# Ten row slots and a step-by-step order in a gather-and-scatter graph network kernel

## The reference

```
h = relu(layernorm(x))
# layer 1, twice (relu between, log_softmax behind): norm holds edge weight and degrees
out = segment_sum((h @ W)[src] * norm[:, None], dst) + b
x = x + log_softmax(out)
# layer 2
h = relu(layernorm(x))
msg = relu(h[src] + edge_attr @ We + be)
h = h + segment_sum(msg, dst)
x = x + relu(batchnorm(relu(h @ W1 + b1) @ W2 + b2))
```

## Time and profile before

| what | value |
|---|---|
| time, median of 3 executions | 6395.15 us (6393.17 to 6398.4) |
| span of the profiled execution | 7443.2 us |
| GpSimd (POOL) busy | 4606.9 us, 62% |
| TensorE (PE) busy | 3143.2 us, 42% |
| VectorE (DVE) busy | 1940.5 us, 26% |
| ScalarE (ACT) busy | 882.4 us, 12% |
| mean granted TensorE clock | 0.553 of full |
| DMA | 293.10 MB, 39 GB/s |

### The profile page before, as it was taken

The page is one execution under the profiler, slowest core; times in us unless marked ns, Lnnn a source line. Parts: engine busy times, 40 slices in busy tenths (PEclk is TensorE's granted clock), DMA queues, the critical chain, the costliest instruction groups (busy, mean ns, idle before and its releaser), DMA issues.

```text
span 7443.2 us, 65119 instructions
## 1 busy us (share of the span) xinstructions
PE 3143.2 (42%) x13129; PEld 2504.6 (34%) x13130; DVE 1940.5 (26%) x6985; ACT 882.4 (12%) x3744; POOL 4606.9 (62%) x4769
## 2 busy tenths in 40 slices
PE   5333333333333533333333333355555555555556
PEld 5322222222222522222222222243333334333334
DVE  3222222222222322222222222252222222222223
ACT  3100000000000200000000000031111111111113
POOL 3566666666666366666666666656666666666665
PEclk5555555555555555555555555556666555656656
DMA  1111111111111211111111111122222222221111
GB/s 41 50 34 33 34 34 33 34 34 33 34 34 33 55 34 34 33 34 34 33 34 34 34 33 34 34 62 45 47 46 46 45 46 46 46 45 44 44 44 48
DMA packets 227042, 293.10 MB, mean 39 GB/s; under 512 B 97266, under 2 KB 147464, under 8 KB 226889
## 3 DMA queue, kind: packets, MB, share of 16 engines
q0 software_dynamic: 150144, 230.70, 14.8%
q1 hardware_dynamic: 76870, 62.08, 2.9%
HBM read 273.19 MB, written 19.25 MB: 39 GB/s over the span
## 4 chain that ended last, share of the span: by engine, by line
POOL 32%; issue 28%; another core or an unknown queue 14%; PE 11%; DVE 6%; DMA 4%; ACT 3%; DVEq 2%; POOLq 0%; ACTq 0%; SPq 0%
POOL rows_g L404 32%; PE psum L747 8%; DMA rows_g<-table,idx 4%; DVE hot L1044 3%; PE psum L694 1%; ACT rows_g L542 1%; DVEq L261 1%; PE psum L781 1%; ACT idx L523 1%; DVE rows_g L1061 1%; DVE acc L1052 1%; ACT attr L522 0%; PE psum L725 0%; PE psum L864 0%
## 5 line engine op out<-in xcount | busy, mean ns | idle before, releaser
L404 POOL DMA_INDIRECT rows_g<-table,idx x4692 | 4444.1, 947 | 2603.7 <-issue 1331.2
L747 PE MATMUL psum<-hot,rows_g 128*96 128x128 f32 x9384 | 2208.9, 415 | 3997.2 <-DMA rows_g<-table,idx 2231.7
L747 PEld LDWEIGHTS psum<-hot,rows_g 128*96 128x96 f32 x9384 | 1895.5, 266 | 4376.5 <-issue 3038.6
L1052 DVE TENSOR_TENSOR acc<-acc,psum 96x128 f32 x1173 | 332.2, 283 | 4591.9 <-PE psum L747 2411.2
L522 ACT ACTIVATE attr<-edge 128x12 f32 (+1 forms) x1173 | 248.8, 212 | 5844.4 <-PE psum L747 3503.9
L1041 DVE TENSOR_SCALAR hot<-iota,attr 128x128 f32<-128x128 f32 x3128 | 828.6, 355 | 277.5 <-issue 247.5
L736 PE MATMUL psum<-we_blk,eaT 128*128 128x384 f32 (+1 forms) x782 | 533.9, 854 | 140.7 <-ACT eaT L538 95.2
L736 PEld LDWEIGHTS psum<-we_blk,eaT 128*128 128x128 f32 (+1 forms) x782 | 241.1, 329 | 349.7 <-issue 349.7
L1044 DVE TENSOR_SCALAR hot<-iota,attr 128x128 f32<-128x128 f32 x1564 | 324.4, 302 | 103.1 <-issue 103.1
L1061 DVE TENSOR_TENSOR rows_g<-rows_g,psum 128x384 f32<-128x384 f32 x391 | 213.8, 547 | 277.0 <-DMA rows_g<-table,idx 233.6
L542 ACT ACTIVATE rows_g<-rows_g 128x384 f32<-128x384 f32 x391 | 200.6, 513 | 391.4 <-DVE rows_g L1061 317.7
(11 more groups left out here) (136 smaller groups left out, 840.2 us busy)
## 6 DMA issues: line engine op xcount, KB each, us to landing
rows_g<-table,idx POOLq DMA_INDIRECT x4692
ea<-in_edge_attr_dram SPq DMA_DIRECT2D x390, 64.0 KB
table<-tab SPq DMA_DIRECT2D x13, 840.0 KB
tab<-in_x_dram SPq DMA_DIRECT2D x100, 46.9 KB
x_sb<-in_x_dram SPq DMA_DIRECT2D x1, 4200.0 KB
out_dram<-x_sb SPq DMA_DIRECT2D x5, 840.0 KB
x_more<-in_x_dram SPq DMA_DIRECT2D x3, 840.0 KB
table<-tab SPq DMA_DIRECT2D x13, 97.5 KB
```

Source lines behind the costliest of these rows:

```text
L404: pool.indirect_dma_start(out=rows_g[u][0:np_, g * F:(g + 1) * F], out_offset=None, in_=table[p], in_offset=bass.IndirectOffsetOnAxis(ap=i ...
L747: last = pe.matmul(ps_agg[u], rows_g[u][0:np_, g * F:(g + 1) * F], hot[u][0:np_, g, :], start=g == 0, stop=g == G - 1)
L1052: dve.tensor_tensor(a, a, ps_agg[u], ALU.add).then_inc(fast.added, 1)
```

## The change

The slots become `U = 10` for `rows_g`, `attr` and `idx`, and `H = 5` for `hot` and `ea`; `eaT`, its PSUM tile, the products' and the aggregates' banks become two each. To make room, `ea`, `eaT` and one `hot` lie in `x_more_t`, and `far` and `stat` lie in the space of `rows_g`. A class `Step` names the slot, the bank and the count of a step. Loops run over ten steps in place of three, and within them the order goes step by step:

- VectorE: one-hots of step s+3, then (pass 2) the edge term of s, then a window (of s; in pass 2 of s-1). The one-hots of the first three steps come before the loop. `build_hot` has a new wait, for the aggregate of the step five before.
- TensorE, pass 2: transpose of s+3, product of s+2, aggregate of s.
- ScalarE, pass 2: copy of s+2, relu of s, stage of s+9; in all passes the first ten steps are staged ahead of the loop.
- GpSimd and SyncE: loops of ten steps; x is loaded again by 25 DMAs of four columns in place of 100 of one, and the log-softmax columns go four at a time in the first 25 loops.

```diff
-    U = 3
+    U = 10
+    H = 5
+    LA = 3
+    LT, LL = 3, 2
@@
-        ps_agg = [bank[u][0:F, 0:W] for u in range(U)]
-        ps_e = [bank[3 + u][:, 0:G * F] for u in range(U)]
+        ps_agg = [bank[k][0:F, 0:W] for k in range(2)]
+        ps_e = [bank[3 + k][:, 0:G * F] for k in range(2)]
@@
+        class Step:
+            def __init__(self, it, k):
+                self.it, self.u = it + k // U, k % U
+                self.s = it * U + k
+                self.h, self.b = k % H, k % 2
+                self.ith = it * (U // H) + k // H
@@ scalar
+            def stage_first(p):
+                act.wait_ge(fast.agg, U + p * NS)
+                for k in range(U):
+                    stage_fast(p, Step(0, k))
...
+            def gin_iter(it):
+                for k in range(U):
+                    t = Step(it, k)
+                    gin_copy(Step(it, k + LL))
+                    relu_msg(fast, t.s, t.u, EP)
+                    if k >= 1:
+                        stage_fast(2, Step(it, k - 1 + U))
+                stage_fast(2, Step(it, 2 * U - 1))
@@ tensor
+            with pe.Fori(0, ITERS - 1) as it:
+                for k in range(U):
+                    gin_transpose(Step(it, k + LT))
+                    gin_linear(Step(it, k + LL))
+                    aggregate(2, Step(it, k))
@@ vector
-            def build_hot(p, s, u, np_):
-                dve.wait_ge(fast.staged, p * NS + s + 1)
+            def build_hot(p, t):
+                n = p * NS + t.s
+                dve.wait_ge(fast.staged, n + 1)
+                dve.wait_ge(fast.agg, n + 1 + U - H)
@@
-                    for u in range(us):
-                        build_hot(p, s0 + u, u, np_)
-                    for u in range(us):
+                for k in range(LA):
+                    build_hot(p, Step(0, k))
+                def full(it):
+                    w = windows(dve, mybir.EngineType.DVE, it * U, U, win_row)
+                    for k in range(U):
+                        t = Step(it, k)
+                        build_hot(p, Step(it, k + LA))
                         if p == 2:
-                            add_edge_term(fast, s0 + u, it, u, np_)
-                            if u >= 1:
-                                add_window(p, s0 + u - 1, u - 1, w[u - 1])
+                            add_edge_term(fast, t.s, t.it, t.u, t.b, EP)
+                            if k >= 1:
+                                add_window(p, Step(it, k - 1), w[k - 1])
```

More of the change, by code:

```diff
@@ L238, in build_gnn, with last_steps @@
         far_dsum = sem("far_deg_used")
[L239 to L246, removed]
+        USES = [ITERS + (TP > 0)] + [ITERS] * (U - 1)
+        class Step:
[4 more added lines that the diff above has]
+                self.ith = it * (U // H) + k // H
+                self.np_ = TP if isinstance(it, int) and it * U + k == FULL else EP
+        REST = NS - (ITERS - 1) * U
+        def last_steps(ahead=0):
+            return [Step(ITERS - 1, k) for k in range(ahead, REST)]
         def if_far(eng, sweep):
@@ L645, in _ @@
         def _(pe):
-            for r, n in ((fast, U), (slow, 1)):
-                pe.sem_inc(r.agg, n)
-                pe.sem_inc(r.tr, n)
-                pe.sem_inc(r.lin, n)
+            for r in (fast, slow):
+                pe.sem_inc(r.agg, r.rows)
+                pe.sem_inc(r.tr, r.eas)
+                pe.sem_inc(r.lin, r.banks)
             pe.sem_inc(far_used, 1)
@@ L742, in aggregate, with aggregate_pass @@
                 if p < 2:
[L743 removed]
+                    pe.wait_ge(fast_got[t.u], 16 * G * (p * USES[t.u] + t.it + 1))
                 else:
[L745 removed]
+                    pe.wait_ge(fast.relu, t.s + 1)
                 for g in range(G):
[L747 removed]
+                    last = pe.matmul(ps_agg[t.b], rows_g[t.u][0:t.np_, g * F:(g + 1) * F], hot[t.h][0:t.np_, g, :],
                                      start=g == 0, stop=g == G - 1)
                 last.then_inc(fast.agg, 1)
+            def aggregate_pass(p):
+                with pe.Fori(0, ITERS - 1) as it:
+                    for k in range(U):
+                        aggregate(p, Step(it, k))
+                for t in last_steps():
+                    if t.s == NS - 1:
+                        warm(WARM)
+                    aggregate(p, t)
+                pe.wait_ge(fast.added, fast.banks + (p + 1) * NS)
             def sweep(p):
@@ L788, in _ @@
                     transpose_nodes(0, q)
-            with pe.Fori(0, ITERS) as it:
-                for u in range(U):
-                    aggregate(0, it * U + u, it, u, P)
-            warm(WARM)
-            aggregate(0, FULL, ITERS, 0, TP)
-            pe.wait_ge(fast.added, U + NS)
+            aggregate_pass(0)
             if_far(pe, lambda: sweep(0))
@@ L807, in _ @@
                     transpose_nodes(1, q - LAG)
-            with pe.Fori(0, ITERS) as it:
-                for u in range(U):
-                    aggregate(1, it * U + u, it, u, P)
-            warm(WARM)
-            aggregate(1, FULL, ITERS, 0, TP)
-            pe.wait_ge(fast.added, U + 2 * NS)
+            aggregate_pass(1)
             if_far(pe, lambda: sweep(1))
@@ L869, in _ @@
         def _(dve):
-            for r, n in ((fast, U), (slow, 1)):
-                dve.sem_inc(r.added, n)
-                dve.sem_inc(r.msg, n)
+            for r in (fast, slow):
+                dve.sem_inc(r.added, r.banks)
+                dve.sem_inc(r.msg, r.banks)
             steps = [0]
```

311 lines of the change are left out of this document (174 added, 137 removed).

## The result

| | before | new kernel |
|---|---|---|
| median, us | 6393.3 (6 runs, 6392.78 to 6398.4) | 6415.87 (6 runs, 6413.0 to 6420.11) |
| ratio | | 1.0035, 95% interval 1.0024 to 1.0047 |
| passes 0, 1, 2, first to last gather, us (before: in its profile of 7443.2) | 2274.6, 2286.4, 2367.6 | 1965.6, 1963.8, 1973.1 |
| all else in the same profiles, us | 514 | 516 |

The new kernel is slower by 22.6 us. The profile of the kernel before (7443.2 us) and its times here (6393.3) belong to two kinds of session, which experiment 7 and the part on the pauses come back to; the new kernel's profile and times agree, so its passes can be read against its times. The forecast was 6388; the time lies inside the range (6345 to 6425), but above the forecast case's own (6363 to 6412), and on the side that had 0.16.

The account below looks back on a forecast made before the run. It took GpSimd's gathers, issued at their own pace without pauses in ordinary executions, to bound the kernel. Terms: 6395 - 0 (ten slots) - 5 (one-hots beside gathers) - 2 (ends of passes) = 6388 us; range 6345 to 6425.

Parts of the forecast that it names:

- the forecast case: Whole kernel: ordinary executions don't change, since GpSimd already issues at its own pace; 6363 to 6412 us, chance 0.79.
- One-hots beside gathers: GpSimd's gathers beside VectorE's one-hots: shorter groups may save up to 14 us or add about as much; taken as -5.
- rival (b): One-hots on VectorE starve GpSimd's gathers: slower, 6510 to 6627 us, deciding from 64 such steps on; chance 0.07.
- rival (a): GpSimd's pauses are real and gathers quicker without recording: 1063 us go, leaving 5332 us; chance 0.07.
- a burden of the recording: Aggregate counts reaching ScalarE late, up to 5.7 us, taken as caused by profiling and absent from ordinary executions.
- the full 1063: GpSimd's pauses in the three passes of the profile, 1063 us, expected gone from the new kernel's profiled execution.
- Ends of passes: Last step's one-hots, transpose and product made ahead: about 1 us per pass less, taken as -2.
- Loop ends: GpSimd's loops of 40 gathers rather than 12, 114 ends for 390: taken as 0, refetching bounded by 182 us.
- SyncE's queue: Attribute loads as before and 25 loads of x for 100: nothing on the path, 0.
- the register loads: VectorE's load of ten windows once in ten steps: 2.4 us, covered by nine other steps of 5.0 us.
- ScalarE's order: ScalarE's copies, relu and staging, under 1.5 us of 5.0 per step, ten slots staged at a pass's head: cost 0.
- Rival (c): Skewed chain of pass 2 holds TensorE at 5.3 us per step: 117 us more, 6512 us; chance 0.03.

Follow-up runs that it names:

- experiment 7: The new kernel unchanged, run in a session where the kernel before takes 7449.03 us: 7408.53 us, ratio 0.9944.
- Experiment 6: New kernel with one-hot blocks delayed, by a wait for ScalarE's staging in passes 0 and 1, by a statistics operation in pass 2: 6387.1 us, ratio 0.9986.

## Why the prediction was wrong, point by point

**The step that failed** is "One-hots beside gathers ... I take -5", with its bound of 14 us either way. It measured +16 to +19 us in one session (46.1 and 43.6 after, 27.5 before), and all other terms together -1.1 by the medians, so it accounts for the result there; that the 22.6 of the result's own session are the same is borne out by its 46.9 us of excess. The mechanism stood in the text, in this paragraph and in rival (b), which asked for 64 slow gathers and got 418; both were priced wrongly.
- The bound was read from the trace of before: mean minus median, 3 ns x 4692 = 14 us. But that trace is of a session in which late counts move the blocks about. Where nothing is late, the one-hots cost the order of before 27.5, and the new one 44 to 46.
- I asked how many gathers lie beside one-hots, and how long the groups are. What decides is whether a one-hot has been under way for 0.05 to 0.20 us when a gather starts. The step order gave the blocks nearly the same distance to a gather in most steps: in passes 0 and 1 582 of 782 blocks start in the last 0.15 us before a gather, and 171 in the trace of before. Experiment 6 shows it: moving the blocks takes the three passes from 5902.5 to 5871.3 us, 31 less.
- Rival (b) took the longest gather seen, +0.20 us, in every step, for 116 to 232 us. The 418 gathers of over 990 ns, in 1173 steps, lose 0.11 each.
- The threshold for (b), "gathers above 0.96 us on average", was too coarse: 0.954 was enough, since 10 ns x 4692 is 47 us.

**The pauses.** "The ordinary executions take just the time of a kernel whose GpSimd never pauses" was right but for at most 27.5 us: without one-hots the order of before has passes of 1952 us with three slots, and 3 x 1952 + 514 = 6370 is within 2 us of its time. What the one-hots add, 27.5, can hold short pauses beside slow gathers, since no trace of that kernel at 6395 exists. So ten slots bring next to nothing, as forecast; rival (a), 5332 us, is out. The reason given, "a burden of the recording", was wrong. Each timed execution also carries its span, 1.8 us under its time (6420.11 and 6418.3 for the profiled one of the new kernel), and in a session all of them agree: all 15 of the kernel before in one session lie between 7443 and 7451. One chip gave the kernel before 6394.28 in one session and 7493.69 in another, 515 s later. So the late counts belong to the session, not to the recording, nor for good to a chip. By all this I had compared a time of one kind of session with a profile of the other; the timed runs of the profile's own session aren't there to prove it. "In the profiled execution I expect the full 1063 to be gone" held only because that profile came from a session of the first kind; in one of the other kind 40 us go.

**The rest.** "Ends of passes, -2": 6370.88 - 6372.02 = -1.1, within what can be told. Loop ends, SyncE's queue, the register loads and ScalarE's order at 0: inside the passes nothing is waited for on GpSimd but the gap of 0.3, and all else is 516 against 514. A load of ten windows, put at 2.4 us, takes 1.31 (median). Rival (c), TensorE's chain in pass 2 at 5.3 us per step: the passes end at GpSimd's pace, and moving the one-hots later in pass 2 costs nothing, so there was cover.

## What to carry to other kernels

When an engine issues without a pause, what is left to gain or lose is in the duration of its own instructions: compare mean with median, and line the longest up with what the other engines start just before them, single operation by single operation. A regular order makes a small clash happen in every step or in none, so the place of a neighbour is worth a wait that costs nothing. And when a profile and the times differ by a sixth, don't explain the difference away: ask for a profile and times of one session.

## What the runs showed of the hardware

- In the new kernel a gather that starts 0.05 to 0.20 us after a single-input one-hot has started takes 1010 ns in the mean in place of 944 (685 gathers, of which 408 over 990). One that starts 0.00 to 0.05 after it takes 947 (259). In passes 0 and 1 one that starts 0.05 to 0.4 us before a block, with none under way, takes 944 (123), and in the last 0.05 us before it 960 (56).
- A gather that starts 0 to 0.15 us after a block of two-input `scalar_tensor_tensor` operations takes 1488 to 1540 in the mean; beside two-input `tensor_tensor` operations in pass 2 it takes 1025. Up to 0.1 us after a statistics operation over 96 columns that a block follows it takes 1091 to 1118 in the mean (507 gathers), after the same operation with no block behind it 947 (44, up to 0.15 us after).
- GpSimd's pace without a clash is 944 + 304 ns, 1952 us per pass of 1564 gathers, in each of six passes.
- Sessions of 7448 to 7494 us show 16 to 17% more time for the kernel before, at the same pace of gathers between pauses and a like granted clock (0.554 against 0.564 of the kernel before on one chip). What makes the counts late there was not found. Of 521 late ones in the new kernel 213 came while GpSimd stood still and the others while it issued, so it isn't shown that its gathers hold them back.
